# The norm behind the feed-forward layer, made group by group: squares on GpSimd, variances and spreads in turn on TensorE

## The reference

```python
def _forward(x, Wq, Wk, Wv, Wo, bo, ln1_g, ln1_b, W1, b1, W2, b2, ln2_g, ln2_b):
    for i in range(DEPTH):                       # DEPTH = 4
        h = _layernorm(x, ln1_g[i], ln1_b[i])
        x = x + _linear_attn(h, Wq[i], Wk[i], Wv[i], Wo[i], bo[i])
        h = _layernorm(x, ln2_g[i], ln2_b[i])
        x = x + (gelu(h @ W1[i] + b1[i]) @ W2[i] + b2[i])
    return x

h = tower(x)
h = _layernorm(h + attn(h))      # the norm behind the last feed-forward layer
h = _layernorm(h + mixture(h))
```

## Time and profile before

| what | value |
|---|---|
| median of 3 runs | 824.98 us (822.92 to 828.79) |
| profiled execution: its own time | 826.26 us |
| its span in the trace | 824.5 us |
| PE busy | 631.6 us (77%) |
| DVE busy | 576.0 us (70%) |
| ACT busy | 362.3 us (44%) |
| POOL busy | 72.1 us (9%) |
| token part in the trace | from about 630 to 824.5 us |
| mean granted TensorE clock | 0.909 |

### The profile page before, as it was taken

One profiled execution on the slowest core, in us unless ns is written; L12 is line 12 of the kernel. 1 busy time (PEld: TensorE's weight loads), 2 busy tenths in 40 slices (PEclk: granted clock), 3 DMA queues, 4 the chain that ended last, 5 costly groups with the idle time before them and its releaser, 6 DMA issues. The chain is left out here.

```text
span 824.5 us, 25191 instructions
## 1 busy us (share of the span) xinstructions
PE 631.6 (77%) x11575; PEld 444.5 (54%) x11575; DVE 576.0 (70%) x896; ACT 362.3 (44%) x517; POOL 72.1 (9%) x112
## 2 busy tenths in 40 slices
PE   3447997466789992666799937788595899999997
PEld 2335775132477771333777723332434787787854
DVE  6852887699448776996468778988731868567453
ACT  0002545870014555900045545737222677767753
POOL 3601000000300000001100000002000222212200
PEclk9986998699879995999699978999987999999999
DMA  9450000000600000004200000013005000000001
GB/s 241 113 108 20 3 3 2 0 2 2 225 9 3 3 4 0 1 2 139 95 3 3 4 7 2 2 36 133 4 14 185 2 2 1 1 2 1 2 1 26
DMA packets 14809, 28.94 MB, mean 35 GB/s; under 512 B 5664, under 2 KB 6304, under 8 KB 14688
## 3 DMA queue, kind: packets, MB, share of 16 engines
q1 hardware_dynamic: 14416, 26.61, 10.9%
q10 hardware_dynamic: 288, 0.73, 0.3%
HBM read 26.28 MB, written 1.05 MB: 33 GB/s over the span
## 5 line engine op out<-in xcount | busy, mean ns | idle before, releaser
L451 ACT ACTIVATE V<-ps,wts 128x1024 f32<-128x1024 f32 x96 | 101.8, 1111 | 285.7 <-PE ps L900 285.7
L597 DVE BATCH_NORM_STATS2 stats<-V 128x6 f32<-128x512 f32 x192 | 117.9, 676 | 31.9 <-ACT V L451 31.9
L900 PE MATMUL ps<-tab,A 64*128 64x128 f32 x1536 | 106.7, 285 | 28.8 <-DMA V<-in_grid 17.1
L900 PEld LDWEIGHTS ps<-tab,A 64*128 64x128 f32 x1536 | 93.6, 192 | 52.8 <-issue 37.4
L541 DVE STREAM_TRANSPOSE A<-V 128x2048 f32<-128x2048 f32 x48 | 107.2, 2270 | 6.2 <-ACT V L430 6.2
L430 ACT ACTIVATE V<-V,small 128x2048 f32<-128x2048 f32 x48 | 96.1, 2080 | 5.0 <-DVE small L632 5.0
L772 PE MATMUL ps<-A,tab 128*128 128x384 f32 x192 | 68.3, 499 | 33.2 <-DVE A L548 33.2
L760 PE MATMUL ps<-A,tab 32*32 32x512 f32 x1536 | 61.3, 655 | 38.6 <-DVE A L541 38.6
L590 DVE STREAM_TRANSPOSE A<-ps 128x2048 f32<-128x2048 f32 (+1 forms) x27 | 55.4, 2070 | 42.9 <-PE ps L885 42.9
L772 PEld LDWEIGHTS ps<-A,tab 128*128 128x128 f32 x192 | 34.4, 189 | 76.7 <-DVE A L548 62.0
L548 DVE STREAM_TRANSPOSE A<-ps 128x1024 f32<-128x1024 f32 x48 | 56.3, 1210 | 11.2 <-PE ps L760 11.2
(11 more groups left out here) (254 smaller groups left out, 916.1 us busy)
## 6 DMA issues: line engine op xcount, KB each, us to landing
A<-in_modes SPq DMA_DIRECT2D x32, 384.0 KB, 7.0
r_ky<-in_modes SPq DMA_DIRECT2D x16, 384.0 KB, 6.0
V<-in_grid SPq DMA_DIRECT2D x12, 120.0 KB
wl<-in_layers SPq DMA_DIRECT2D x3, 452.0 KB, 5.1
wm<-in_mixture SPq DMA_DIRECT2D x1, 874.5 KB, 7.5
tab<-in_table SPq DMA_DIRECT2D x1, 656.5 KB, 4.7
A<-in_turned SPq DMA_DIRECT2D x1, 512.0 KB, 3.6
tower_out<-A SPq DMA_DIRECT2D x4, 128.0 KB, 2.3
```

The lines of the kernel that those rows point to most:

```text
L451: nc.scalar.activation(Vm[:, 2 * h:2 * h + 2, r, 512 * q:512 * (q + 1)], bank(half_of_u(q, r) + 2 * h, 2).rearrange("p (m n) -> p m n", m= ...
L597: last = nc.vector.bn_stats(stats[:, 16 * q + 4 * r + m, :], Vm[:, m, r, 512 * q:512 * (q + 1)])
L900: last = nc.tensor.matmul(ps[:, at:at + P], G[(2 * q + quad) % 4][rows, x:x + P], inv_y[rows, :], start=step < 2 and quad == 0, stop=step ...
```

## The change

Behind the feed-forward layer, in all four layers:

- The squares move from ACT to POOL, where a new semaphore `s_sqp` counts them. ACT keeps the very first norm's squares and those behind attention.
- PE computes the variance of group 0 ahead of the last group's feed-forward matmuls. Behind them it takes in turn the variance of group g and the spreading of group g-1. The spreading of group 3 stands behind group 0's projections of the next layer (behind the fourth layer: directly behind the others).
- DVE takes the reciprocal of group 0 ahead of the last sum, and then in turn a reciprocal and the product of the group ahead.
- In the last layer POOL computes `zb` (x plus the tower's output) before these squares, as it did before.

The norm ahead of layer 1 and the three others behind attention keep their order. The line numbers of the new file are larger by up to 33 behind the edits.

```diff
@@ gpsimd
+            def square(l):
+                for g in range(G):
+                    pool.wait_ge(s_x, (2 * l + 1) * G + g + 1)
+                    nc.gpsimd.tensor_tensor(part(sqT, g), part(xT, g), part(xT, g), ALU.mult).then_inc(s_sqp, 1)
...
+                square(l)
@@ scalar
             for l in range(DEPTH):
                 preload(ACT.Sqrt)
-                square(l, 0)
+                if l == 0:
+                    square(0, 0)
                 deviation(2 * l, s_var, s_ln)
...
             preload(ACT.Sqrt)
-            for g in range(G):
-                act.wait_ge(s_x, (2 * DEPTH - 1) * G + g + 1)
-                nc.scalar.activation(part(sqT, g), part(xT, g), ACT.Square).then_inc(s_zsq, 1)
-            deviation(0, s_zvar, s_zdev)
+            deviation(2 * DEPTH, s_var, s_ln)
@@ vector
+            def residual_and_norm(l):
+                n = 2 * l + 2
+                for g in range(G - 1):
+                    add_up(l, 1, g, s_ff2, 0)
+                reciprocal(n, 0)
+                add_up(l, 1, G - 1, s_ff2, 0)
+                for g in range(1, G):
+                    reciprocal(n, g)
+                    scale(n, g - 1)
+                scale(n, G - 1)
...
             for l in range(DEPTH):
-                scaled(l, 0)
                 if l == 0:
+                    scaled(0, 0)
                     centre_layer(0)
...
-                residual(l, 1, s_ff2, 0)
+                residual_and_norm(l)
@@ tensor
+            def variance_behind(l, g):
+                pe.wait_ge(s_sqp, l * G + g + 1)
+                token_variance(g).then_inc(s_var, 1)
+
+            def norm_behind(l):
+                for g in range(1, G):
+                    variance_behind(l, g)
+                    spread_of(2 * l + 2, g - 1)

             for l in range(DEPTH):
                 w = wl[:, l, :]
-                variance(l, 0)
+                if l == 0:
+                    variance(0, 0)
                 pe.wait_ge(s_wl[l], 16)
                 for g in range(G):
+                    if l and g == 1:
+                        spread_of(2 * l, G - 1)
                     pe.wait_ge(s_h, 2 * l * G + g + 1)
...
                     last.then_inc(s_ff2, 1)
+                    if g == G - 2:
+                        variance_behind(l, 0)
+                norm_behind(l)
+
+            spread_of(2 * DEPTH, G - 1)
```

More of the change, by code:

```diff
@@ L1160, in token_kernel @@
         s_sq = sem("s_sq")
+        s_sqp = sem("s_sqp")
         s_var = sem("s_var")
@@ L1189, in token_kernel @@
         s_ff2 = sem("s_ff2")
[L1190 to L1194, removed]
         s_nT = sem("s_nT")
@@ L1294, in _ @@
                                                     ALU.mult).then_inc(s_qn, 1)
-            for g in range(G):
-                pool.wait_ge(s_x, (2 * DEPTH - 2) * G + g + 1)
-                nc.gpsimd.tensor_tensor(part(zb, g), part(xT, g), part(u0T, g), ALU.add).then_inc(s_zb, 1)
+                if l == DEPTH - 1:
+                    for g in range(G):
+                        pool.wait_ge(s_x, (2 * DEPTH - 2) * G + g + 1)
+                        nc.gpsimd.tensor_tensor(part(zb, g), part(xT, g), part(u0T, g), ALU.add).then_inc(s_zb, 1)
+                square(l)
         @block.scalar
@@ L1424, in centre_layer, with reciprocal, scale @@
                     last.then_inc(s_wcen, 1)
+            def reciprocal(n, g):
+                dve.wait_ge(s_ln, n * G + g + 1)
+                nc.vector.reciprocal(rdev[:, GT * g:GT * (g + 1)], dev[:, GT * g:GT * (g + 1)]).then_inc(s_r, 1)
+            def scale(n, g):
+                dve.wait_ge(s_rb, n * G + g + 1)
+                if n == 2 * DEPTH:
+                    nc.vector.tensor_tensor(part(hT, g), part(xT, g), bank(g, 0), ALU.mult).then_inc(s_nT, 1)
+                else:
+                    nc.vector.tensor_tensor(part(h0T, g), part(xT if n else u0T, g), bank(g, 0), ALU.mult).then_inc(s_h0, 1)
@@ L1426, in scaled @@
             def scaled(l, which):
                 for g in range(G):
-                    n = 2 * l + which
-                    dve.wait_ge(s_ln, n * G + g + 1)
-                    nc.vector.reciprocal(rdev[:, GT * g:GT * (g + 1)], dev[:, GT * g:GT * (g + 1)]).then_inc(s_r, 1)
+                    reciprocal(2 * l + which, g)
                 for g in range(G):
-                    dve.wait_ge(s_rb, n * G + g + 1)
-                    nc.vector.tensor_tensor(part(h0T, g), part(xT if n else u0T, g), bank(g, 0), ALU.mult).then_inc(s_h0, 1)
+                    scale(2 * l + which, g)
@@ new lines, in add_up @@
+            def add_up(l, which, g, done, b):
+                dve.wait_ge(done, l * G + g + 1)
+                last_one = l == DEPTH - 1 and which
+                if last_one:
+                    dve.wait_ge(s_zb, g + 1)
+                nc.vector.scalar_tensor_tensor(out=part(xT, g), in0=bank(g, b), scalar=bcol[:, 2 * l + which:2 * l + which + 1],
+                                               in1=part(zb if last_one else xT if l or which else u0T, g),
+                                               op0=ALU.add, op1=ALU.add).then_inc(s_x, 1)
@@ L1435, in residual @@
             def residual(l, which, done, b):
                 for g in range(G):
[L1437 to L1443, removed]
+                    add_up(l, which, g, done, b)
@@ L1607, in spread_over_features, with spread_of, variance @@
                 return last
-            def variance(l, which):
-                n = 2 * l + which
+            def spread_of(n, g):
+                pe.wait_ge(s_r, n * G + g + 1)
+                spread_over_features(g).then_inc(s_rb, 1)
+            def variance(n, squares):
                 for g in range(G):
-                    pe.wait_ge(s_sq, n * G + g + 1)
+                    pe.wait_ge(s_sq, squares * G + g + 1)
                     token_variance(g).then_inc(s_var, 1)
                 for g in range(G):
-                    pe.wait_ge(s_r, n * G + g + 1)
-                    spread_over_features(g).then_inc(s_rb, 1)
+                    spread_of(n, g)
+            def variance_behind(l, g):
[5 more added lines that the diff above has]
+                    spread_of(2 * l + 2, g - 1)
             for l in range(DEPTH):
                 w = wl[:, l, :]
-                variance(l, 0)
+                if l == 0:
+                    variance(0, 0)
                 pe.wait_ge(s_wl[l], 16)
                 for g in range(G):
+                    if l and g == 1:
+                        spread_of(2 * l, G - 1)
                     pe.wait_ge(s_h, 2 * l * G + g + 1)
@@ L1667, in _ @@
                     nc.tensor.matmul(bank(g, 1), w[:, W_O:W_O + P], part(oT, g), start=True, stop=True).then_inc(s_wo, 1)
-                variance(l, 1)
+                variance(2 * l + 1, l + 1)
                 for g in range(G):
```

## The result

| kernel | median | runs | mean granted clock in the profile |
|---|---|---|---|
| before | 827.6 us (819.73 to 832.2) | 20 | 0.909 |
| changed | 832.4 us (825.24 to 840.51) | 20 | 0.898 |

The ratio of the changed kernel to the one before is 1.0063, 95% interval 1.004 to 1.0087. The profiled execution of the changed kernel took 832.63 us (span 830.8). The forecast was 820.5 us, range 817.8 to 825.5.

What follows compares the result with a forecast made beforehand. The norm was taken as bound by TensorE's queue and what it waits for. Three layers gaining 2.8 us in all plus 1.7 at the mixture made 4.5; 824.98 - 4.5 gave 820.5 us, range 817.8 to 825.5.

Steps and rivals of the forecast that it cites:

- The idle 0.47 us: TensorE's idle time between the last feed-forward matmul and the first variance; forecast to go.
- Squares: Squares behind the feed-forward layer on GpSimd: 0.65 us, the last one covered by 0.6 us, so costing nothing.
- The table load: ScalarE's Sqrt table, 1.28 us, forecast to delay little; rival that it arrives late: 824.3 us, chance 0.04.
- E: Old end of the last feed-forward matmul ahead of the norm: start of these matmuls plus 3.67 us.
- TensorE's queue: Norm's matmuls in turn without waits, variance 0.47 and spread 0.48 us each; group 0's projections end at E + 4.64.
- group 1's maximum: VectorE's start on group 1 in the next layer: E + 7.09 instead of 8.02, gaining 0.93 us a layer.
- the mixture's start: First mixture matmul behind the fourth norm: E + 4.5 instead of 6.18, gaining 1.7 us.
- the step on the clock: Assumed TensorE's upper clock level throughout the new norm, granted clock 1.00 as behind attention.
- a fall: A stretch with TensorE's clock at its lower level (1.2 GHz, not 2.4); priced at 1.71 us each in the norm.
- the wait of VectorE for spread 3: Product 3 needs spread 3 and stands ahead of the next layer's first maximum, which starts at E + 5.77.
- The clock still falls: Rival: clock falls between variance 1 and spread 3, 1.71 us each; four give 827.3 us; three or four, chance 0.12.
- The remark that they also come elsewhere: Noted for the clock rival: the clock also falls in unexplained places outside the norm, as at 723 us.

Runs made afterwards that it cites:

- numbers 1 and 7: 1: old order without the tower, four layers run twice, 347.23 us. 7: the same with the transposes of the exponentials issued twice, 339.88 us.
- The two comparisons: Whole changed kernel against the kernel before: first 832.4 us, ratio 1.0063; once more on the same chip 828.44 us, ratio 1.0026.

## Why the prediction was wrong

**Right.** The idle 0.47 us went. Squares take 0.61 us and are covered. The table load delays nothing: reciprocal 0 ended at E + 0.48, forecast 0.49. The load takes 1.28 us, as forecast; the drain that the Trainium skill (ScalarE: Activation LUTs, "What ACT_TABLE_LOAD costs") puts beside the load shows in none of these traces as a wait behind it. The clock stayed up in all four norms.

**Mis-sized: TensorE's queue.** I took the prices of a variance and a spread from blocks of 16 and 32 records. In blocks of 4 and 8 the first matmul of each block comes late: the load of its weights doesn't start ahead of it (0.17 us idle ahead of a variance's or projection's load). It isn't the semaphores: the old blocks wait for one in each group too, and run through without a gap. It comes where TensorE turns from one kind of matmul to another. Each turn costs about 0.1 us. Eight blocks (variance 0, the last feed-forward group, three variances, three spreads) make it 0.68: projections 0 started at E + 3.99 instead of 3.31. They took 0.20 more themselves, and group 1's maximum came at 7.87 instead of 7.09. Measured by the old 8.02 the gain was 0.15 us for a layer, not 0.93, and the mixture's start, at 4.94 instead of 4.5, gained 1.24, not 1.7.

**Failed: the step on the clock.** "All these prices assume the upper level" was said of the new kernel, while the old one's 8.02 us contained a fall. I booked its end as a gain of the change. Without a fall the old order's maximum comes at 6.48 and its mixture starts at 4.56 (numbers 1 and 7): by my own sum, 7.09 and 4.5, the change would have lost 0.61 us in each layer and gained 0.06 at the mixture. The fall itself I priced at 1.71 us; it costs the maximum 1.54. And falls are not the norm's own: the experiments show that they come about as often in either order and cost as much. With the transposes twice, and where no fall is left, a passage takes 33.51 us in the old order and 34.89 in the change; without that, the means are 35.12 and 36.39. So falls cost 1.61 us a passage there and 1.50 here. They left the norm (1.54 us) and came back in attention. What remains is the order at equal clock: 34.89 - 33.51 = 1.38 us slower in a passage, and 4.94 - 4.56 = 0.38 at the mixture. The maximum was the right thing to read: without a fall it is 23.4 us from group 1's maximum to the next layer's second feed-forward matmuls in both orders, with the squares alone and with spread 3 ahead, and 7.87 - 6.48 makes up the whole 1.38. Only, it has to be compared at the same clock.

**Where the 1.38 us come from.** Spread 3 ahead of projections 0 takes the passage to 33.91: 0.98 us are the wait of VectorE for spread 3, which I had seen, but priced against an old norm with a fall in it. Squares alone, at 32.99, are 0.52 better than the old order. The turns on TensorE and VectorE with variance 0 moved ahead cost 33.91 - 32.99 = 0.92 against that.

**The sum, corrected.** 3 x 1.27 - 1.24 = 2.6 us slower. The 1.24 at the mixture is a fall that went (1.62) less the order's own 0.38. The two comparisons gave 1.0063 and 1.0026; 2.6 us are 1.0031, inside the second interval and just below the first. What made the first comparison larger by some 2.5 us isn't known.

**Rivals.** "The clock still falls" gave 827.3 us and the right sign, but that was luck, for it had the wrong place: it put the falls into the norm, where there were none. The remark that they also come elsewhere was in it; I didn't ask what follows if they move.

**Open.** What makes the clock fall. Why spread 3 ahead and product 3 later escape nearly all falls, and the squares alone don't, isn't known: TensorE's gaps between the transposes are the same in all three, one of 0.89 us and the others of 0.22 or so. The change itself differs from them, it has two long gaps (0.84 and 0.88 us); whether the second one brings on its falls wasn't tested apart. Filling the gap in the norm with matmuls, and nothing else, wasn't tried; the squares alone close it, and there the falls go from the norm and come in attention.

## What to carry to other kernels

Compare an order with another at the same clock: take the duration of a stretch where the clock was up in both, and treat falls as a cost of the whole loop; here they moved to another place when one gap was closed. Taking turns group by group pays only where an engine waits; here each turn cost TensorE 0.1 us, and VectorE's last product, which had to wait for its spread, stood in front of work that was ready. One part of this change, the squares on an idle engine, gained alone what the whole lost.

## What the runs showed that I had not expected

- More matmuls made the kernel faster: eight more transposes a layer, 7 to 10 us in all (354.3 to 344.8, 347.2 to 339.9, 337.6 to 329.8).
- A wait of VectorE for one group was worth 1 us in its place and another 1.4 us in the clock (36.39 to 34.02 a passage, with the maximum only 0.99 earlier).
- Up to the same instruction, layer 1's second feed-forward matmuls, the kernel before took 664.16 us in one profile and 668.03 in another, more than the change is worth.
